# Layer 1's recurrence: scores made and masked in two halves of two PSUM banks

## What is computed

```python
def _L1_attn_ref(hidden_states, ...):
    q, k, v = (conv_silu(hidden_states @ w) ...)      # 8 heads of 16 features
    beta = sigmoid(hidden_states @ b_w)
    q, k = _l2norm(q), _l2norm(k)
    attn = inverse of (I + strictly lower part of (k*beta) @ k.T), in chunks of 32 tokens
    u, w = attn @ (v * beta), attn @ (k * beta)
    def step(S, inp):                                  # over the chunks
        qi, ki, ui, wi = inp
        attn_i = jnp.where(tri_incl, qi @ jnp.swapaxes(ki, -1, -2), 0.0)
        ui = ui - wi @ S
        oi = qi @ S + attn_i @ ui
        S = S + jnp.swapaxes(ki, -1, -2) @ ui
        return (S, oi)
    g = sigmoid(hidden_states @ mix_w + mix_b + mix_bias)
    o = g * o + (1.0 - g) * v
    o = o * rsqrt(mean(o * o)) * o_norm_w
    return o @ o_w
```

## Time and profile before

| | us |
|---|---|
| runs of the kernel | 2538.8, 2542.91, 2543.85 (median 2542.91) |
| the profiled execution | 2544.81 |
| span of its trace | 2543.0 |
| `delta_outputs`, from its first matmul (703.43) to the end of its last sum on DVE (760.82 + 0.42) | 57.8 |
| of these, from `score(0)` (707.45) | 53.8 |

### The profile page before, as it was taken

The page is one execution under the profiler, slowest core; times in us unless marked ns, Lnnn a source line. Parts: engine busy times, 40 slices in busy tenths (PEclk is TensorE's granted clock), DMA queues, the critical chain, the costliest instruction groups (busy, mean ns, idle before and its releaser), DMA issues. The chain is left out here.

```text
span 2543.0 us, 36807 instructions
## 1 busy us (share of the span) xinstructions
PE 1891.2 (74%) x11751; PEld 1125.9 (44%) x11763; DVE 1741.1 (68%) x5543; ACT 1137.8 (45%) x3143; POOL 711.8 (28%) x620
## 2 busy tenths in 40 slices
PE   6996889854868999979987876665655565555777
PEld 2654447442445666654454554333333333333443
DVE  4326342277755656647745677999999999995655
ACT  3652542242315666641142564555455555554421
POOL 1200045014422333320022420444333343332130
PEclk8988889966988999989988897666666666666979
DMA  5000101400000000000010000000000000000000
GB/s 209 2 1 1 43 12 31 160 1 1 2 2 1 1 2 0 1 1 0 23 71 1 1 1 0 1 1 1 1 0 1 1 1 1 1 1 1 1 1 17
DMA packets 10591, 37.76 MB, mean 15 GB/s; under 512 B 1344, under 2 KB 7488, under 8 KB 9136
## 3 DMA queue, kind: packets, MB, share of 16 engines
q1 hardware_dynamic: 8880, 33.04, 3.3%
q0 software_dynamic: 1536, 2.59, 0.4%
HBM read 30.15 MB, written 5.51 MB: 14 GB/s over the span
## 5 line engine op out<-in xcount | busy, mean ns | idle before, releaser
L3702 PE MATMUL psum<-work 32*128 32x256 f32 x512 | 131.7, 660 | 290.4 <-ACT work L3812 290.4
L3871 DVE MATCH_REPLACE8 work<-work 128x256 f32<-128x256 f32 x768 | 306.5, 414 | 0.0
L3919 POOL TENSOR_TENSOR work<-work 128x1024 f32<-128x1024 f32 x64 | 150.6, 2354 | 494.3 <-ACT work L3812 494.3
L3868 DVE MAX8 work<-work 128x8 f32<-128x256 f32 x768 | 267.8, 415 | 0.0
L3702 PEld LDWEIGHTS psum<-work 32*128 32x128 f32 x512 | 78.4, 314 | 317.5 <-ACT work L3812 162.9
L702 POOL TENSOR_TENSOR work<-work 128x256 f32<-128x256 f32 (+2 forms) x144 | 133.3, 944 | 252.9 <-DVE work L980 252.9
L910 ACT ACTIVATE work<-work 128x128 f32<-128x128 f32 (+1 forms) x320 | 144.9, 454 | 41.6 <-PE psum L767 22.9
L3812 ACT ACTIVATE work<-work 128x256 f32<-128x256 f32 x256 | 128.4, 502 | 0.0
L3725 PE MATMUL psum<-work,tiles 128*8 128x256 f32 x512 | 117.3, 611 | 13.7 <-ACT work L3821 13.7
L3921 POOL TENSOR_TENSOR work<-work 128x1024 f32<-128x1024 f32 x64 | 121.1, 1892 | 6.1 <-DVE work L3893 1.2
L3810 ACT ACTIVATE work<-psum,work 128x256 f32<-128x256 f32 x256 | 117.4, 459 | 0.0
(11 more groups left out here) (616 smaller groups left out, 4652.1 us busy)
## 6 DMA issues: line engine op xcount, KB each, us to landing
big_weights<-L0f_dram SPq DMA_DIRECT2D x1, 6117.5 KB, 29.3
big_weights<-L_dram SPq DMA_DIRECT2D x1, 5772.0 KB, 17.5
big_weights<-L_dram SPq DMA_DIRECT2D x1, 4952.5 KB, 16.0
choice_rows<-tiles SPq DMA_DIRECT2D x2, 1024.0 KB, 10.7
tiles<-choice_rows SPq DMA_DIRECT2D x8, 256.0 KB, 5.1
big_weights<-L_dram SPq DMA_DIRECT2D x1, 2027.0 KB, 21.3
big_weights<-L_dram SPq DMA_DIRECT2D x1, 1630.5 KB, 13.7
big_weights<-L0f_dram SPq DMA_DIRECT2D x1, 1630.5 KB, 6.4
```

Source lines behind the costliest of these rows:

```text
L3702: mm = nc.tensor.matmul(scores(n)[:, u, :], qb[head, tile % 2, u % 2 * P:(u % 2 + 1) * P], kb[head, tile % 2, :], start=True, stop=True, t ...
L3868: ch.step(v.max(top8[:, n % 2, u, r, :], src[:, u, :]))
L3871: ins = v.match_replace(raw[:, n % 2, u, :], top8[:, n % 2, u, r, :], src[:, u, :], REPLACED)
L3919: ch.link(g.tensor_tensor(mine, mine, rest[:, n % 2], ALU.subtract))
```

## The change

`score(n)` is made in two halves. The first half is bands 0 and 1 (banks 0 and 1), the second bands 2 and 3 (banks 2 and 3). Each half has its own wait for the mask of the unit before and its own signal. The mask is two instructions of 768 columns instead of one of 1536, the first on banks 0 and 1, the second on banks 2 and 3, each waiting for its half of the scores and signalling by itself. So `score(n)`'s first half waits only for the first mask of unit n-1. `mix(n)` waits for both masks of unit n.

```diff
-                if n >= 1:
-                    pe.wait_ge(c.scores_masked.sem, c.scores_masked.at(n))
-                for j in range(4):
-                    nc.tensor.matmul(scores(j)[:, 0:3:2, :], k[band[j], b * S:b * S + P], src[band[j], b * S:(b + 1) * S],
-                                     start=True, stop=True, tile_position=(32 * j, 0))
-                for j in range(4):
-                    mm = nc.tensor.matmul(scores(j)[:, 1, :], k[band[j], b * S + P:(b + 1) * S],
-                                          src[band[j], b * S + P:(b + 1) * S], start=True, stop=True,
-                                          tile_position=(32 * j, 0))
-                mm.then_inc(c.scores_ready.sem, 1)
+                for half in range(2):
+                    if n >= 1:
+                        pe.wait_ge(c.scores_masked.sem, c.scores_masked.at(2 * n - 1 + half))
+                    for j in (2 * half, 2 * half + 1):
+                        nc.tensor.matmul(scores(j)[:, 0:3:2, :], k[band[j], b * S:b * S + P], src[band[j], b * S:(b + 1) * S],
+                                         start=True, stop=True, tile_position=(32 * j, 0))
+                    for j in (2 * half, 2 * half + 1):
+                        mm = nc.tensor.matmul(scores(j)[:, 1, :], k[band[j], b * S + P:(b + 1) * S],
+                                              src[band[j], b * S + P:(b + 1) * S], start=True, stop=True,
+                                              tile_position=(32 * j, 0))
+                    mm.then_inc(c.scores_ready.sem, 1)
...
-                pe.wait_ge(c.scores_masked.sem, c.scores_masked.at(n + 1))
+                pe.wait_ge(c.scores_masked.sem, c.scores_masked.at(2 * n + 2))
...
-                    dve.wait_ge(c.scores_ready.sem, c.scores_ready.at(n + 1))
                     if n >= 2:
                         dve.wait_ge(c.mixed_ready.sem, c.mixed_ready.at(n - 1))
-                    v.tensor_tensor(probs[n % 2], c.psum[:, 0:4, 0:3 * P].rearrange("p j (a x) -> p j a x", x=P),
-                                    masks[:, b % 4].unsqueeze(1).broadcast_to([P, 4, 3, P]), ALU.mult) \
-                        .then_inc(c.scores_masked.sem, 1)
+                    for half in range(2):
+                        two = slice(2 * half, 2 * half + 2)
+                        dve.wait_ge(c.scores_ready.sem, c.scores_ready.at(2 * n + half + 1))
+                        v.tensor_tensor(probs[n % 2][:, two], c.psum[:, two, 0:3 * P].rearrange("p j (a x) -> p j a x", x=P),
+                                        masks[:, b % 4].unsqueeze(1).broadcast_to([P, 2, 3, P]), ALU.mult) \
+                            .then_inc(c.scores_masked.sem, 1)
```

More of the change, by code:

```diff
@@ L2754, in _ @@
             ch.clear()
-    for s, n in ((c.updates_moved, 4), (c.updates_placed, 4), (c.scores_ready, len(units)), (c.scores_masked, len(units)),
+    for s, n in ((c.updates_moved, 4), (c.updates_placed, 4), (c.scores_ready, 2 * len(units)),
+                 (c.scores_masked, 2 * len(units)),
                  (c.mixed_ready, len(units)), (c.out_copied, B), (c.out_turned, B), (c.heads_scaled, B), (c.gated, B),
```

## The result

| | us |
|---|---|
| the changed kernel, median of 21 runs | 2538.18 (2532.3 to 2543.5) |
| the kernel before, median of 21 runs beside it | 2542.39 (2537.4 to 2547.2) |
| ratio | 0.9983, interval 0.9977 to 0.9990 |
| profiled execution after | 2540.51, span 2538.7 |

The change saves 4.2 us or 0.17%. The interval excludes a ratio of 1, so the kernel is faster, but by less than the 0.2% that the prediction drew as its bound. The interval runs from 2.5 to 5.8 us; it holds the 3.6 as well as the 5.4 us of the prediction's two accounts, so what decides between them is the length of the block in the traces, not the time of the program. Forecast were 2537.5 us and a range of 2534 to 2544.

A forecast was written before the change was run, and what follows sets the result against it. PE and DVE were taken to idle in turn in a ring of score and mask. Savings of 3.85 + 2.9 + 0.57 = 7.3 us off the profiled 2544.8 gave 2537.5 us, range 2534 to 2544.

The forecast's parts named there:

- the prediction's two accounts: PE's low clock in the block either stays (3.6 us saved) or goes (7.3 saved, 5.4 below the median of before).
- The ring and its new period: Score and mask wait for each other over the same banks; a two-unit sequence at full clock goes from 5.63 to 4.90 us.
- The layout without a fall: Block with PE's clock staying full: scores A of units 2 to 6 at 711.98 to 723.58, 3.85 us less by score(6).
- The half mask, 0.96: On DVE, a mask of 768 columns takes 0.96 us (0.88 to 1.10); the second half begins 0.87 after the first.
- The half score as long as a whole: On PE, a half takes 1.00 us to its mask; the second half is free beside the first where nothing holds it.
- the 0.1 that was given as a sign: Sign of being right: in even units the eight matmuls of L2654 begin within 0.1 us.
- The two `place` on the path: Two `place` on PE (1.71 and 0.89 us), formerly under a mask, now take back the gain in units three and five.
- Without it 7.3. I expect it to go: The fall of PE's clock at 710.6 us vanishes as its preceding idle time shrinks, saving 7.3 us; forecast's chance 0.45.
- the term of 3.85 us: Start of the block, score(0) to score(6): 3.85 us less if the clock doesn't fall, 0.16 if it does.
- Rival 1: The fall of PE's clock in the 710s stays while the ring shortens: 3.6 us less, 2541.2; chance 0.26.
- Rivals 2 to 4: Halves run one after another (0.17); narrower work keeps PE's clock low, slower (0.06); half mask costs 1.10 (0.06, shared).
- Rival 2: On PE, the second half starts 0.75 us after the first unforced: sequence 5.17, time 2539.7 or 2544.7; chance 0.17.

The follow-up runs named there:

- the third trace: The changed kernel traced a third time, nothing else changed: a block of 46.6 us, no low clock up to the last unit.
- the experiment with the scores alone: Kernel before with only the score's matmuls reordered (bands 0 and 1 first), one whole mask, no wait between: sequence 5.70 us, one execution 2535.8 us.
- second trace of before: The kernel before, unchanged, traced again for its clock: a block of 50.9 us, no low clock up to the last unit.
- the later comparisons: The changed kernel timed against the kernel before in two more comparisons: ratios 0.9981 (0.9970 to 0.9991) and 0.9985 (0.9975 to 0.9995).

## Why the prediction was right or wrong

**The ring and its new period: right.** The sum rested on a sequence of 4.90 us; it is 4.92 in all four traces of the change. Each step was within 0.04. The layout without a fall adds up to 16.13 + 4 x 4.90 + 10.72 = 46.5 us from score(0) to the last sum; the third trace, which had the full clock to the last unit, has 46.6.

**The half mask, 0.96: right**, it is 0.95, and two cost 1.82. **The half score as long as a whole, and two of them side by side where nothing holds them: right** (score(6) above, and the experiment with the scores alone). The eight records of L2654 begin within 0.35 us there and not within the 0.1 that was given as a sign: each matmul is two records, and it is the first ones of the four bands that begin together. **The two `place` on the path: right.** Score A of units 5 and 6 is 3.74 us apart in the changed kernel (722.76 and 726.50) with a `place` between, and 2.88 without one (728.55 and 731.43); before it was 2.90 (724.53 to 727.43) against 2.81.

**"Without it 7.3. I expect it to go": wrong.** This is the step that failed. In the sum it stands in the term of 3.85 us for score(0) to score(6). That term measured 2.2 in the profiled execution. At the full clock in both kernels it is 1.0 (17.05 against 16.09 us, second trace of before and third of the change); the other 2.9 are the fall that the one profiled execution of before happened to have (19.98 against 17.05). Taken off 7.3 it leaves some 4.3 us, which is what the block gains at the full clock (50.9 to 46.6) and about what the program gains (4.2, and by the ratios 4.8 and 3.8 in the later comparisons). The cause of the fall was read from the idle time ahead of it, and the runs contradict this twice: the fall stays away with the same 1.88 us idle, and comes with 0.16. Other executions of the kernel before have none, those of the changed kernel have some. Rival 1 (3.6 less, 2541.2) had the better account of the mechanism: 3.5 measured with equal low clock. It too took a fall as given.

**The time was right partly by luck.** 7.3 us were taken off the profiled execution, which was 1.9 above the median, and this made 5.4 off the median where 4.2 were measured. The 5.4 lie within the interval of 2.5 to 5.8 us, so the program's time does not refute them; what the traces refute is the account behind them.

**Rivals 2 to 4** are out by themselves: halves side by side, no lasting low clock (1.00 from 716.8 to 752 though PE works in halves), half masks at 0.95. (For matmuls in strict order the prediction's part on the score in two points at the third rival; the second is meant.) Rival 2's mechanism is real when it is forced, at 5.8 us a sequence.

**Not seen: that a third of the mask's work was a product with one.** The ring's longest member could be cut, not only split.

## What to carry to other kernels

Where two engines take turns on one buffer, lay out the ring of waits, with every instruction that the change puts into it, with durations from the trace: it gave the period within 0.02 us, and showed that PE's own row would end last, so that halving a 1.76 us stage brought 0.36 a unit and not 0.9. Ask what the longest member does before splitting it: a block with a constant mask needs no multiplication, and an idle engine can copy it. A stretch of low clock in one profile is one draw; price a change at equal clock first, and trace a few more executions before counting a fall as lost or saved or giving it a cause.

## What was not expected of the hardware

- Matmuls of different row groups begin in another order than the program lists them: with bands 2 and 3 listed behind both widths of bands 0 and 1, all wide ones still ran in one burst of 0.73 us, at a cost of 0.02 to 0.04 a unit.
- A wait of PE for its own last matmul leaves it idle for 0.16 us beyond the matmul's end as the profile has it; DVE, waiting for the same signal, starts 0.04 us before PE.
- The low clock came in pieces of 3.4, 6.8, 10.2 or 13.6 us at places that differed between executions of one program. It fell behind a stretch in which PE had been busy for 2.90 of 3.20 us, and did not fall in an execution with 1.88 us of idle PE.
- DVE (banks 0 and 1) and ACT (banks 2 and 3) reading PSUM at the same time slowed neither: 0.69 us for 512 columns as in the earlier trace rows, and 0.37 for ACT's 256, as for its copy of 256 columns at 756.50 in the kernel before, when DVE stood idle.
